# Turning one quadrant of w1 on VectorE instead of TensorE in a two-layer LoRA kernel on one core, with two adapter products and x's rows in another order

## The chip, the cores and the metric

One core of a Trainium2 chip runs the program. The metric is the device time in microseconds (us), median of several executions. The program is one launch, and all arithmetic of the reference is done on the core.

## The reference

Two residual linear layers follow each other, each with a low-rank adapter picked by an index; x is 8 x 256 x 1024 in float32.

```
x = x + x @ W0.T + (x @ lora_A[label]) @ lora_B.T * 0.5
x = x + x @ W1.T + bias + (x @ lora_As[slot]) @ lora_Bs[slot] * 2
```

The layers have 1024 inputs and outputs. The adapter ranks are 32 and 16.

## The kernel before, in words

**One matrix for two layers.** With an identity added to each weight (a for W0, b for W1 turned over), the two layers are one product with V = a·b plus low-rank terms. The kernel first makes V, once, and then takes 8 batches of 256 rows of x through it. Both the making of V and the batches use a Winograd-type scheme over 2 x 2 quadrants of 512 x 512: sums S1 to S4 of a's quadrants, T1 to T4 of b's, seven products of which each is `row_product` or `by_halves`. In the trace the sums and their parts are s, t, the results v, vt, m.

**Three products for one.** Each float32 operand is split in a high part, which ScalarE makes by a rounding copy (`high`), and a low part, which VectorE makes as a difference (`low`). TensorE then does hi·hi, hi·lo and lo·hi, each a 128x512 matmul (`step`, L1262 on).

**b's quadrants have to be turned.** w1 lies as rows of outputs, and b11, b12, b22 and b21 are wanted with inputs on the partitions. `turn` (L1217) does it with four 128x128 transposes on TensorE for each 128 columns, into a bank of PSUM; ScalarE and VectorE read the bank. b21 is the last: `turn_b21` is called three times between the halves of the product S2·T2 and once within the second half (L1352 to L1356). From the bank ScalarE copies `b21_hi` and `b21` (L543 to L546), VectorE makes `b21_lo` (`b21_low`, L898).

**The order ahead of the product A12·B21.** After S2·T2 TensorE runs, in this order: q's first half with B21, the adapter's c with A11 and A12 (`c_first`), b0·a1 (8 matmuls with 256 columns), and q's second half with T3 and B22. All orders are written out by hand, engine by engine, with semaphores between them. The order on VectorE at that place is `a1_lo`, `a1d`, two `b21_low`, `t4_sum(0)`, two `b21_low`, four `low` of a12, `t4_sum(1)`, and so on.

**Where the later steps meet.** ScalarE takes c's first half out of PSUM (`ct`), then makes `s1_hi` twice, then takes out b0·a1 (`q_part`); VectorE sums that into `b0a1_all` and goes on with `s1_low`. Further on, four rounds of `vt23(m)` (vt2, then vt3) and `turn_x` follow on VectorE. ScalarE makes vt2_hi and vt3_hi of each round and only after the last one copies c's second half (`ct[:, H:D]`), which TensorE waits for (`ct_made`, 2) after the first quarter of S1·T1, before it turns ct. In batch 0, TensorE waits for `u_lo_made` (`u_low` on VectorE) before the product with `p_hi` that adds the low-rank term.

**x's rows.** `turn_x` (L962) turns x by 32x32 blocks on VectorE; row 8·sl + 2·sb + odd of a batch goes to column 4·sl + sb of `xt`, so that a block of 32 results is written with a step of four elements. The store puts partition p to row 2·p + odd.

```
nc.vector.transpose(xt[:, n, :, :].rearrange("p e (s sb) -> p sb e s", sb=GR).bitcast(I32),
                    rows[:, n // 2, n % 2].bitcast(I32)).then_inc(xt_made, 1)
```

**Loads.** All are on SyncE's queue, in order: the quadrants of w1 and W0 in pairs, then n21 (raw w1 quadrant 21, 4 DMAs with pieces of 512 bytes), a12, a1 (8 DMAs, one per batch, after the index is known), a0, and x once `q_done` is 1.

Of the kernel before, what the change touches and what calls it, by code (L numbers as in the profile page):

```python
# [5 lines left out]
F32 = mybir.dt.float32  # L6
# [14 lines left out]
def two_layer_lora_kernel(nc, x, label0, slot1, w0, a0, b0w, w1, bias, a1, b1, out):  # L21
# [45 lines left out]
    n21 = at("n21", [P, HK, HK, P], F32, 20 * SLOT)  # L67
# [84 lines left out]
    with ExitStack() as ctx:  # L152
        bank = [ctx.enter_context(nc.psum_tensor(f"bank{n}", [P, 512], F32)) for n in range(8)]

        def sem(name):
            return ctx.enter_context(nc.semaphore(name))
# [4 lines left out]
        n21_in = [sem(f"n21_in{j}") for j in range(HK)]  # L161
# [27 lines left out]
        T22_AT, T12_AT, T21_AT = (4, 5, 8, 9), (6, 7, 10, 11), (12, 13, 14, 15)  # L189
# [47 lines left out]
        TURN_BANK = [bank[n] for n in (6, 7, 4, 5, 6, 7, 4, 5, 6, 7, 4, 6, 7, 4, 6, 7)]  # L237
        TURNED_THERE = {4: 0, 5: 1, 6: 2, 7: 3, 8: 4, 9: 5, 10: 6, 11: 8, 12: 9, 13: 10, 14: 11, 15: 12}
# [16 lines left out]
        def last_half(h):  # L255
            dst = out[B - 1, :, sides[h]].rearrange("(p odd) i -> odd p i", odd=2)
            return dst[0], y[:, C11, sides[h]]
# [6 lines left out]
        def _(sp):  # L264
# [201 lines left out]
        def _(act):  # L466
# [94 lines left out]
            for h in range(2):  # L561
                high(b22_hi, b22, PAIR[h], w1_hi_made)
# [153 lines left out]
        def _(dve):  # L716
# [144 lines left out]
            def t4_sum(h):  # L861

                dve.wait_ge(t2_made, h + 1)
                dve.wait_ge(w1_made, 2 * HK + 2 * h + 2)
                tt(t4[:, PAIR[h], :], b21[:, PAIR[h], :], t2[:, PAIR[h], :], ALU.subtract, t4_made)
# [24 lines left out]

            raw_a1 = a1_raw[:, :, :, :].rearrange("p t b r -> p t (b r)")
# [4 lines left out]
            tt(a1d[:, :, :], raw_a1[:, HK:KT, :], raw_a1[:, 0:HK, :], ALU.subtract, a1d_made)  # L896

            def b21_low(j):  # L898
                dve.wait_ge(w1_made, 2 * HK + j + 1)
                tt(b21_lo[:, j, :], TURN_BANK[T21_AT[j]][:, :], b21_hi[:, j, :].bitcast(F32), ALU.subtract, w1_lo_made)  # L900

            b21_low(0)
            b21_low(1)
            t4_sum(0)
            b21_low(2)
            b21_low(3)
# [3 lines left out]
            t4_sum(1)  # L910
            q_half(0)
            b22_low(0)
            b22_low(1)
# [20 lines left out]
            p_low(1)  # L934
# [15 lines left out]
            v11_sum(0)  # L950
            a22_low(0)
            a22_low(1)
            v11_sum(1)
            v11_sum(2)
# [5 lines left out]
            for m in range(HK):  # L960
                v11_low(m)
# [240 lines left out]
        def _(pe):  # L1202
# [8 lines left out]
            def row_tile(tile, j, m):  # L1211
# [4 lines left out]
                     + [(t1_made, 1), (t1_made, 2)] + [(w1_made, HK + 3), (w1_made, HK + 4)]  # L1216
                     + [(t1_made, 3), (t1_made, 4)] + [(w1_lo_made, HK + 1)])  # L1217
# [154 lines left out]
            for j in range(HK):  # L1372
                q_step(Q_BANK[1], j, T3, j, j == 0, False)
            pe.wait_ge(w1_lo_made, 2 * HK + 2)
            for j in range(HK):
                last = q_step(Q_BANK[1], KT + j, B22, j, False, j == HK - 1)
            last.then_inc(q_done, 1)
# [222 lines left out]
```

## Time and profile before

| what | value |
|---|---|
| median of 3 runs | 294.67 us (294.54 to 294.78) |
| the profiled execution, device time | 294.32 us |
| its span, first to last instruction | 292.6 us |
| granted TensorE clock, mean | 1.000 |
| TensorE matmul busy | 288.8 us, 99% |
| VectorE busy | 242.8 us, 83% |
| ScalarE busy | 153.9 us, 53% |
| GpSimd busy | 30.4 us, 10% |
| HBM read, written | 20.59 MB, 8.39 MB |

A timeline row gives the start in us from the span's start, the length in us, engine, line, operation, output<-input by name, and the idle time before it with what ended it. Matmuls overlap: a 128x512 one is shown with 0.39 us, and the next one starts 0.23 us after it. On VectorE and ScalarE too the next instruction starts some 0.1 us before the shown end of the last, if it waits for nothing.

### The profile page before, as it was taken

How to read it: one execution, taken by the hardware profiler on the slowest of the kernel's cores; microseconds unless marked ns; L12 is line 12 of the kernel's file. 1: busy time of each engine (PE TensorE's matmuls, PEld its weight loads, DVE VectorE, ACT ScalarE, POOL GpSimd, SP SyncE). 2: the span in 40 equal slices, each digit the busy share in tenths (PEclk: the TensorE clock that was granted, in tenths of full speed). 3: DMA queues.
4: the chain of work that ended last, by engine and by line, in shares of the span. 5: the costliest groups of instructions: out<-in, count | busy, mean ns of one | idle time of the engine just before them, and what ended most of it. 6: DMA issues, size and time to landing. Idle time of an engine off the chain costs nothing.

```text
span 292.6 us, 4450 instructions
## 1 busy us (share of the span) xinstructions
PE 288.8 (99%) x1337; PEld 236.0 (81%) x1337; DVE 242.8 (83%) x368; ACT 153.9 (53%) x270; POOL 30.4 (10%) x81
## 2 busy tenths in 40 slices
PE   8999999999999999999999999999999999999996
PEld 6888888888888888878878878878878878878885
DVE  3789996999999999999996897797798698695432
ACT  3685576879257537464453463373364355355120
POOL 1718100010000501000100100100100100100000
DMA  6999420800006600093268076068068159013004
GB/s 203 323 322 325 51 37 10 137 1 2 0 0 110 98 27 1 5 148 136 46 100 217 22 130 188 18 103 220 3 108 214 16 103 237 0 36 145 0 1 146
DMA packets 100803, 29.17 MB, mean 100 GB/s; under 512 B 85548, under 2 KB 93996, under 8 KB 100788
## 3 DMA queue, kind: packets, MB, share of 16 engines
q1 hardware_dynamic: 100788, 28.99, 42.7%
q8 instruction: 7, 0.11, 0.2%
q14 instruction: 8, 0.07, 0.1%
HBM read 20.59 MB, written 8.39 MB: 99 GB/s over the span
## 4 chain that ended last, share of the span: by engine, by line
PE 99%; ACT 0%; DVE 0%; issue 0%
PE bank L1204 94%; PE bank L1228 3%; PE bank L1450 1%; PE bank L1416 0%; ACT b_hi L468 0%; DVE y L718 0%
## 5 line engine op out<-in xcount | busy, mean ns | idle before, releaser
L1204 PE MATMUL bank<-v_hi,lhs 128*128 128x512 f32 (+1 forms) x136 | 42.5, 377 | 0.0
L1204 PE MATMUL bank<-vt_hi,s_hi 128*128 128x512 f32 x96 | 37.3, 389 | 0.0
L1204 PE MATMUL bank<-vt_lo,s_hi 128*128 128x512 f32 x96 | 37.3, 389 | 0.0
L1204 PE MATMUL bank<-vt_hi,s_lo 128*128 128x512 f32 x96 | 37.3, 389 | 0.0
L969 DVE STREAM_TRANSPOSE xt<-raw 128x512 int32<-128x512 int32 x32 | 32.4, 1076 | 1.4 <-DMA raw<-in_x 1.4
L1204 PEld LDWEIGHTS bank<-v_hi,lhs 128*128 128x128 f32 x136 | 25.1, 188 | 4.5
L468 ACT ACTIVATE lhs<-xt 128x512 fp32r<-128x512 f32 x32 | 19.6, 626 | 13.0 <-PE bank L1204 12.7
L1204 PE MATMUL bank<-v_lo,lhs 128*128 128x512 f32 (+1 forms) x68 | 25.7, 378 | 0.0
L1204 PE MATMUL bank<-vt_hi,lhs 128*128 128x512 f32 x64 | 22.1, 406 | 0.0
L718 DVE TENSOR_TENSOR lhs<-xt,lhs 128x512 fp32r<-128x512 f32 x32 | 21.7, 686 | 0.3
L434 POOL CAST ac<-c_hi 128x128 fp32r (+1 forms) x16 | 7.2, 450 | 135.5 <-PE bank L1204 98.5
L718 DVE TENSOR_TENSOR s_lo<-s_sum,s_hi 128x512 fp32r<-128x512 f32 x32 | 21.1, 682 | 0.2 <-ACT s_hi L468 0.2
L1204 PEld LDWEIGHTS bank<-vt_lo,s_hi 128*128 128x128 f32 x96 | 18.0, 188 | 3.7
L1204 PEld LDWEIGHTS bank<-vt_hi,s_hi 128*128 128x128 f32 x96 | 18.0, 188 | 3.7
L1204 PEld LDWEIGHTS bank<-vt_hi,s_lo 128*128 128x128 f32 x96 | 18.0, 188 | 3.7
L468 ACT ACTIVATE s_hi<-s_sum 128x512 fp32r<-128x512 f32 x32 | 19.1, 624 | 2.1 <-DVE s_sum L718 1.8
L1204 PE MATMUL bank<-t_hi,s_hi 128*128 128x512 f32 x48 | 19.1, 397 | 0.0
L1204 PE MATMUL bank<-t_hi,s_lo 128*128 128x512 f32 x48 | 18.7, 390 | 0.0
L1204 PE MATMUL bank<-t_lo,s_hi 128*128 128x512 f32 x48 | 18.7, 389 | 0.0
L468 ACT ACTIVATE u_part<-bank 64x256 f32<-64x256 f32 x8 | 3.1, 382 | 28.0 <-PE bank L1204 28.0
L718 DVE TENSOR_TENSOR y<-bank,u_sum 128x512 f32<-128x512 f32 x16 | 11.0, 685 | 6.3 <-PE bank L1204 6.3
L468 ACT ACTIVATE vt_hi<-vt 128x512 fp32r<-128x512 f32 x16 | 10.1, 630 | 10.9 <-DVE vt L718 10.5
(167 smaller groups left out, 662.6 us busy)
## 6 DMA issues: line engine op xcount, KB each, us to landing
raw<-in_x SPq DMA_DIRECT2D x32, 256.0 KB, 4.9
out<-y SPq DMA_DIRECT2D x31, 256.0 KB, 2.7
n<-in_L_cond_W SPq DMA_DIRECT2D x16, 256.0 KB, 5.3
a<-in_L_cond_W SPq DMA_DIRECT2D x16, 256.0 KB, 5.2
a_raw<-in_L_cond_lora_A SPq DMA_DIRECT2D x8, 128.0 KB, 2.4
b_raw<-in_L_cond_lora_Bs SPq DMA_DIRECT2D x16, 64.0 KB, 2.1
e_raw<-in_L_cond_lora_Bs SPq DMA_DIRECT2D x32, 32.0 KB, 1.8
a_raw<-in_L_cond_lora_As SPq DMA_DIRECT2D x8, 64.0 KB, 2.4
```

Of the source, the lines that this page charges most:

```text
L434: nc.gpsimd.tensor_copy(ac[:, :, at_col:at_col + R1], c_hi[:, :, cols].bitcast(F32)).then_inc(ac_c_made, 1)
L468: nc.scalar.activation(out_ap, in_ap, COPY, scale=scale).then_inc(made, 1)
L718: nc.vector.tensor_tensor(out_ap, one, other, op).then_inc(made, 1)
L969: nc.vector.transpose(xt[:, n, :, :].rearrange("p e (s sb) -> p sb e s", sb=GR).bitcast(I32), rows[:, n // 2, n % 2].bitcast(I32)).then_in ...
L1204: return nc.tensor.matmul(ps, lhsT, rhs, start=start, stop=stop, skip_group_check=more)
L1228: last = nc.tensor.transpose(ps[:, P * t:P * t + P], tile[:, j, t, :], eye[:, :])
L1450: return nc.tensor.matmul(ps, e_st[rows, P * t:P * t + P], e_p[rows, cols], start=False, stop=True, skip_group_check=True, tile_position=( ...
```

## The change

w1's quadrant 21 is loaded by 16 DMAs instead of 4, in pieces of 32 numbers (128 bytes), so that groups of 32 columns stand on the partitions that they need; four transposes by 32x32 blocks on VectorE then give b21. TensorE's 16 transposes and ScalarE's four copies `b21` are gone. `b21_low` reads b21 in place of a bank. On TensorE q's second half with T3 goes ahead of q's first half with B21, and the one with B22 goes between the two halves of c, all ahead of b0·a1. a1 is loaded ahead of a12. On VectorE both `t4_sum` stand after the first `v11_sum`, `a1d` after a12's lows, `p_low(1)` after `v11_sum(0)`, vt2's first sum ahead of v11's lows. x's rows go to columns 32·sb + sl instead of 4·sl + sb, and the stores put them back with a matching pattern.

```diff
-            for j in range(HK):
-                load_n(n21, 0, 1, j, n21_in[j])
-            for j in range(HK):
-                load_a(a12, 0, 1, j, a12_in[j])
+            w1_21 = w1[0:H, H:D].rearrange("(nb sl) (j g r) -> j g sl nb r", sl=32, g=GR, r=32)
+            for j in range(HK):
+                for g in range(GR):
+                    sp.dma_start(n21[32 * g:32 * g + 32, j, :, :], w1_21[j, g]).then_inc(n21_in, 16)
...
+            for j in range(HK):
+                load_a(a12, 0, 1, j, a12_in[j])
...
-                    "o (p odd) i -> odd (o p) i", odd=2)
+                    "o (sl sb odd) i -> odd (o sb) sl i", sb=GR, odd=2)
...
+            for j in range(HK):
+                act.wait_ge(w1_made, 2 * HK + j + 1)
+                high(b21_hi, b21, j, w1_hi_made)
             act.wait_ge(a1_in, 16 * B)
             copy(a1_hi[:, :, :], a1_raw[:, :, :, :].rearrange("p t b r -> p t (b r)"), a1_hi_made, LORA1_SCALE)
-            for j in range(HK):
-                act.wait_ge(turned, T21_AT[j] + 1)
-                bank_copy(b21_hi, j, TURN_BANK[T21_AT[j]], w1_hi_made)
-                bank_copy(b21, j, TURN_BANK[T21_AT[j]], w1_made)
             act.wait_ge(v_done, M6 + HK)
+            for h in range(2):
+                high(b22_hi, b22, PAIR[h], w1_hi_made)
...
+            dve.wait_ge(n21_in, 64 * HK)
+            dve.wait_ge(v_done, M7 + HK)
+            for j in range(HK):
+                nc.vector.transpose(b21[:, j, :].bitcast(I32),
+                                    n21[:, j, :, :].rearrange("p nb r -> p (nb r)").bitcast(I32)).then_inc(w1_made, 1)
...
-                    nc.vector.transpose(xt[:, n, :, :].rearrange("p e (s sb) -> p sb e s", sb=GR).bitcast(I32),
+                    nc.vector.transpose(xt[:, n, :, :].rearrange("p e (sb s) -> p sb e s", sb=GR).bitcast(I32),
...
-                    if h == 1 and m == 2:
-                        turn_b21(HK - 1)
-                if h == 0:
-                    for j in range(HK - 1):
-                        turn_b21(j)
+            pe.wait_ge(t1_made, HK)
+            pe.wait_ge(w1_made, 2 * HK)
+            for j in range(HK):
+                q_step(Q_BANK[1], j, T3, j, j == 0, False)
             for j in range(HK):
                 pe.wait_ge(w1_lo_made, HK + j + 1)
                 last = q_step(Q_BANK[0], HK + j, B21, j, False, j == HK - 1)
             last.then_inc(q_done, 1)
             pe.wait_ge(a1_lo_made, 1)
-            pe.wait_ge(w1_made, 3 * HK)
             c_first(0, A11)
+            pe.wait_ge(w1_lo_made, 2 * HK + 2)
+            for j in range(HK):
+                last = q_step(Q_BANK[1], KT + j, B22, j, False, j == HK - 1)
+            last.then_inc(q_done, 1)
             pe.wait_ge(w0_lo_made, 2 * HK)
             c_first(1, A12).then_inc(ct_done, 1)
```

VectorE, from the last low part of S2 to the sums of b0·a1, before (b_58 is b21, n_69 is n21, t_75 T2, t_81 T4, s_93 S4, b_64 b22, a_55 a12; a_st is a1_lo):

```order
L718 TENSOR_TENSOR s_lo<-s_87,s_hi 128x1024
L893 SCALAR_TENSOR_TENSOR a_st<-a_raw,a_st 128x8x128
L718 TENSOR_TENSOR a1d<-a_raw 128x512
L718 TENSOR_TENSOR b_lo<-bank,b_hi 128x512 x2
L718 TENSOR_TENSOR t_81<-b_58,t_75 128x1024
L718 TENSOR_TENSOR b_lo<-bank,b_hi 128x512 x2
L718 TENSOR_TENSOR a_lo<-a_55,a_hi 128x512 x4
L718 TENSOR_TENSOR t_81<-b_58,t_75 128x1024
```

The same place now:

```order
L720 TENSOR_TENSOR s_lo<-s_87,s_hi 128x1024
L896 STREAM_TRANSPOSE b_58<-n_69 128x512 x4
L720 TENSOR_TENSOR b_lo<-b_58,b_hi 128x512 x4
L909 SCALAR_TENSOR_TENSOR a_st<-a_raw,a_st 128x8x128
L720 TENSOR_TENSOR b_lo<-b_64,b_hi 128x1024 x2
L720 TENSOR_TENSOR a_lo<-a_55,a_hi 128x512 x4
L720 TENSOR_TENSOR a1d<-a_raw 128x512
```

Four transposes have come in, and the two sums T4 have gone from here. VectorE again, from q's second half to the first round of vt, now (v_99 is V11, vt_110 vt2, vt_113 vt3):

```order
L806 SCALAR_TENSOR_TENSOR q<-bank,q_part 32x512
L720 TENSOR_TENSOR s_lo<-s_93,s_hi 128x1024 x2
L720 TENSOR_TENSOR v_99<-bank,m_96 128x512
L720 TENSOR_TENSOR p_hi<-q,p_hi 32x512
L720 TENSOR_TENSOR t_81<-b_58,t_75 128x1024 x2
L720 TENSOR_TENSOR v_99<-bank,m_96 128x512 x2
L720 TENSOR_TENSOR a_lo<-a_61,a_hi 128x1024 x2
L720 TENSOR_TENSOR t_lo<-t_72,t_hi 128x1024 x2
L720 TENSOR_TENSOR v_99<-bank,m_96 128x512
L720 TENSOR_TENSOR t_lo<-t_81,t_hi 128x1024 x2
L720 TENSOR_TENSOR vt_110<-bank,m_97 128x512
L720 TENSOR_TENSOR v_lo<-v_99,v_hi 128x512 x4
```

Both sums T4 now stand behind the first v_99, and the four v_lo behind the first vt_110; what follows is as before.

## Rows read from the trace of the kernel before

**Rows 1.** The page: span, and the chain that ended last.

```profile
span 292.6 us, 4450 instructions
...
PE 99%; ACT 0%; DVE 0%; issue 0%
```

**Rows 2.** Waits of TensorE: who waited for whom, us in total, times, longest.

```profile
PE bank L1204 <- PEq L1589: 0.8, 1, 0.8
```

**Rows 3.** Timeline of TensorE around b21's transposes; start us, length us.

```profile
39.74 1.47 PE L1228 MATMUL bank<-eye,n 128*128 128x128 f32 x12
40.97 0.48 PE L1204 MATMUL bank<-t_hi,s_hi 128*128 128x512 f32 x1
...
45.19 0.60 PE L1228 MATMUL bank<-eye,n 128*128 128x128 f32 x4
45.54 0.48 PE L1204 MATMUL bank<-t_hi,s_hi 128*128 128x512 f32 x1
45.86 0.39 PE L1204 MATMUL bank<-t_lo,s_hi 128*128 128x512 f32 x1
```

**Rows 4.** Timeline of VectorE, from S2's last low part to the fourth round of vt.

```profile
38.82 1.23 DVE L718 TENSOR_TENSOR s_lo<-s,s_hi 128x1024 fp32r<-128x1024 f32 x1
...
43.09 1.22 DVE L718 TENSOR_TENSOR t<-b,t 128x1024 f32<-128x1024 f32 x1
...
58.00 0.27 DVE L923 SCALAR_TENSOR_TENSOR b0a_all<-bank,q_part 32x128 f32<-32x128 f32 x1
...
65.84 2.36 DVE L718 TENSOR_TENSOR a_lo<-a,a_hi 128x1024 fp32r<-128x1024 f32 x2 [0.68 <-ACT a_hi L468]
...
74.46 2.49 DVE L718 TENSOR_TENSOR v_lo<-v,v_hi 128x512 fp32r<-128x512 f32 x4
...
82.70 1.08 DVE L969 STREAM_TRANSPOSE xt<-raw 128x512 int32<-128x512 int32 x1
83.64 0.67 DVE L718 TENSOR_TENSOR vt<-bank,m 128x512 f32<-128x512 f32 x1
84.34 0.69 DVE L718 TENSOR_TENSOR vt<-vt,v 128x512 f32<-128x512 f32 x1
```

**Rows 5.** Timeline of TensorE: b0·a1, start of A12·B21, ct's transposes.

```profile
54.27 1.12 PE L1204 MATMUL bank<-a_st,b_st 128*128 128x256 f32 x8
...
58.88 0.39 PE L1204 MATMUL bank<-b_hi,a_hi 128*128 128x512 f32 x1
...
88.80 1.03 PE L1416 MATMUL bank<-eye,ct 128*128 128x128 f32 x8
```

**Rows 6.** Timeline of ScalarE at c's two halves.

```profile
54.53 0.60 ACT L468 ACTIVATE ct<-bank 128x512 f32<-128x512 f32 x1 [0.91 <-PE bank L1204]
...
57.05 0.27 ACT L468 ACTIVATE q_part<-bank 32x128 f32<-32x128 f32 x1
...
84.34 1.36 ACT L468 ACTIVATE vt_hi<-vt 128x512 fp32r<-128x512 f32 x2 [0.89 <-DVE vt L718]
86.28 0.60 ACT L468 ACTIVATE ct<-bank 128x512 f32<-128x512 f32 x1 [0.57 <-PE bank L1204]
```

**Rows 7.** Timeline of VectorE in batch 0, up to u_low.

```profile
116.60 0.42 DVE L718 TENSOR_TENSOR u_sum<-bank,u_part 64x256 f32<-64x256 f32 x1 [0.32 <-ACT u_part L468]
...
117.39 1.08 DVE L969 STREAM_TRANSPOSE xt<-raw 128x512 int32<-128x512 int32 x1
118.50 0.42 DVE L718 TENSOR_TENSOR u_st<-u_sum,u_st 32x256 fp32r<-32x256 f32 x1
...
123.66 0.48 DVE L1057 SCALAR_TENSOR_TENSOR u_st<-hh,low_mask,u_sum 32x256 fp32r<-32x256 f32 x1
```

**Rows 8.** Timeline of TensorE in batch 0: the product that waits for u_low.

```profile
124.29 0.63 PE L1204 MATMUL bank<-p_hi,u_st 128*128 128x512 f32 x2
```

**Rows 9.** Timeline of SyncE's issues: n21, x.

```profile
18.55 3.25 SPq L272 DMA_DIRECT2D n<-in_L_cond_W  x4
...
49.02 6.30 SPq L305 DMA_DIRECT2D raw<-in_x  x4
```

More of the change, by code:

```diff
@@ L66, in two_layer_lora_kernel @@
     n11 = at("n11", [P, HK, HK, P], F32, 12 * SLOT)
-    n21 = at("n21", [P, HK, HK, P], F32, 20 * SLOT)
+    n21 = at("n21", [P, HK, H // 32, 32], F32, 20 * SLOT)
     n22 = at("n22", [P, HK, HK, P], F32, 16 * SLOT)
@@ L160, in two_layer_lora_kernel @@
         n11_in = [sem(f"n11_in{j}") for j in range(HK)]
-        n21_in = [sem(f"n21_in{j}") for j in range(HK)]
+        n21_in = sem("n21_in")
         n22_in = [sem(f"n22_in{j}") for j in range(2)]
@@ L183, in two_layer_lora_kernel @@
         c_hi_made, c_lo_made = sem("c_hi_made"), sem("c_lo_made")
-        T22_AT, T12_AT, T21_AT = (4, 5, 8, 9), (6, 7, 10, 11), (12, 13, 14, 15)
+        T22_AT, T12_AT = (4, 5, 8, 9), (6, 7, 10, 11)
         n_eyed, w0_eyed, turned = sem("n_eyed"), sem("w0_eyed"), sem("turned")
@@ L235, in two_layer_lora_kernel @@
         HIGH = [bank[5], bank[4], bank[7], bank[6]]
-        TURN_BANK = [bank[n] for n in (6, 7, 4, 5, 6, 7, 4, 5, 6, 7, 4, 6, 7, 4, 6, 7)]
-        TURNED_THERE = {4: 0, 5: 1, 6: 2, 7: 3, 8: 4, 9: 5, 10: 6, 11: 8, 12: 9, 13: 10, 14: 11, 15: 12}
+        TURN_BANK = [bank[n] for n in (6, 7, 4, 5, 6, 7, 4, 5, 6, 7, 4, 6)]
+        TURNED_THERE = {4: 0, 5: 1, 6: 2, 7: 3, 8: 4, 9: 5, 10: 6, 11: 8}
         Q_BANK = [bank[5], bank[6]]
@@ L255, in last_half @@
         def last_half(h):
-            dst = out[B - 1, :, sides[h]].rearrange("(p odd) i -> odd p i", odd=2)
+            dst = out[B - 1, :, sides[h]].rearrange("(sl sb odd) i -> odd sb sl i", sb=GR, odd=2)
             return dst[0], y[:, C11, sides[h]]
@@ L560, in _ @@
             q_half(0)
-            for h in range(2):
-                high(b22_hi, b22, PAIR[h], w1_hi_made)
             act.wait_ge(a1d_made, 1)
@@ L863, in t4_sum @@
                 dve.wait_ge(t2_made, h + 1)
-                dve.wait_ge(w1_made, 2 * HK + 2 * h + 2)
+                dve.wait_ge(w1_lo_made, HK + 2 * h + 2)
                 tt(t4[:, PAIR[h], :], b21[:, PAIR[h], :], t2[:, PAIR[h], :], ALU.subtract, t4_made)
@@ L889, in _, with b21_low @@
                 s2_low(h)
+            dve.wait_ge(n21_in, 64 * HK)
[3 more added lines that the diff above has]
+                                    n21[:, j, :, :].rearrange("p nb r -> p (nb r)").bitcast(I32)).then_inc(w1_made, 1)
+            def b21_low(j):
+                dve.wait_ge(w1_hi_made, HK + j + 1)
+                dve.wait_ge(w1_made, 2 * HK + j + 1)
+                low(b21_lo, b21, b21_hi, j, w1_lo_made)
+            for j in range(HK):
+                b21_low(j)
             raw_a1 = a1_raw[:, :, :, :].rearrange("p t b r -> p t (b r)")
@@ L895, in _ @@
                                            op1=ALU.subtract).then_inc(a1_lo_made, 1)
[L896 to L906, printed above, removed]
+            b22_low(0)
+            b22_low(1)
             for j in range(HK):
@@ L909, in _ @@
                 low(a12_lo, a12, a12_hi, j, w0_lo_made)
-            t4_sum(1)
+            tt(a1d[:, :, :], raw_a1[:, HK:KT, :], raw_a1[:, 0:HK, :], ALU.subtract, a1d_made)
             q_half(0)
-            b22_low(0)
-            b22_low(1)
             s4_sum(0)
@@ L933, in _ @@
                 low(s4_lo, s4, s4_hi, PAIR[h], vs_lo_made)
-            p_low(1)
             def t1_low(h):
@@ L950, in _ @@
             v11_sum(0)
+            p_low(1)
+            t4_sum(0)
+            t4_sum(1)
+            v11_sum(1)
+            v11_sum(2)
             a22_low(0)
             a22_low(1)
-            v11_sum(1)
-            v11_sum(2)
             t1_low(0)
@@ L959, in _ @@
             t4_low(1)
-            for m in range(HK):
-                v11_low(m)
             def turn_x(b, quarters):
@@ L968, in turn_x, with vt2_sum @@
                 for n in quarters:
-                    nc.vector.transpose(xt[:, n, :, :].rearrange("p e (s sb) -> p sb e s", sb=GR).bitcast(I32),
+                    nc.vector.transpose(xt[:, n, :, :].rearrange("p e (sb s) -> p sb e s", sb=GR).bitcast(I32),
                                         rows[:, n // 2, n % 2].bitcast(I32)).then_inc(xt_made, 1)
-            def vt23(m):
+            def vt2_sum(m):
                 dve.wait_ge(v_done, M3 + m + 1)
@@ L976, in vt23, with vt3_sum @@
                 tt(vt2[:, m, :], HIGH[m][:, :], m17[:, m, :], ALU.add, vt2_made)
+            def vt3_sum(m):
                 dve.wait_ge(vt2_made, m + 1)
@@ L986, in vt23_low @@
                 low(vt3_lo, vt3, vt3_hi, m, vt3_lo_made)
+            vt2_sum(0)
+            for m in range(HK):
+                v11_low(m)
             dve.wait_ge(q_done, 2)
             for m in range(HK):
-                vt23(m)
+                if m:
+                    vt2_sum(m)
+                vt3_sum(m)
                 turn_x(0, (m,))
@@ L1215, in _ @@
             taken = ([(w1_made, j + 1) for j in range(HK)] + [(w1_made, HK + 1), (w1_made, HK + 2)]
-                     + [(t1_made, 1), (t1_made, 2)] + [(w1_made, HK + 3), (w1_made, HK + 4)]
-                     + [(t1_made, 3), (t1_made, 4)] + [(w1_lo_made, HK + 1)])
+                     + [(t1_made, 1), (t1_made, 2)] + [(w1_made, HK + 3), (w1_made, HK + 4)])
             def turn(tile, j, n, eyed=0):
@@ L1241, in turn_b12 @@
                 turn(n12, j, T12_AT[j])
-            def turn_b21(j):
-                pe.wait_ge(n21_in[j], 16)
-                turn(n21, j, T21_AT[j])
             def step(ps, a, b, j, m, start, stop, more=False):
@@ L1371, in _ @@
             last.then_inc(b0a1_done, 1)
-            for j in range(HK):
[L1373 to L1377, printed above, removed]
             for m in range(HK):
```

## The prediction, made before the changed kernel had run

> **What bounds the kernel now.** I read the page first: TensorE is the whole chain that ended last, 99% [rows 1]. Then its waits: 0.8 us, at the very start [rows 2]. So TensorE never waits, and its idle time tells nothing; what counts is the distance from one matmul's start to the next. From the start of A12·B21 to the transposes of ct stand 132 matmuls of 128x512, in 88.80 - 58.88 = 29.92 us [rows 5], 0.227 us each: a stream without a gap. Whatever leaves this stream is gained, whatever makes it wait is lost one for one, so I look for the instruction of another engine that TensorE would now meet. Those are in the timelines of VectorE and ScalarE [rows 4, 6, 7]. VectorE waits little between 40 and 116 us: it is nearly as full there as TensorE is.
>
> The profiled execution took 294.32 us for a span of 292.6 us; the median of the runs is 294.67. All shifts below are against the profiled execution's own times, and I add their sum to the median.
>
> **1. The transposes leave TensorE.** The first twelve take from 39.74 to 40.97, 1.23 us; four more take 45.19 to 45.54, 0.35 us; after each of the two groups the first matmul holds the stream 0.32 us (45.54 to 45.86) in place of 0.227, 0.09 more [rows 3]. Sum 1.23 + 0.35 + 0.18 = 1.76 us gained.
>
> **2. The cover that they gave.** The second half of S2·T2 waits for S2's last low part, which ends on VectorE at 38.82 + 1.23 = 40.05 [rows 4]. It was hidden behind the twelve transposes; now TensorE stands there at 39.74. With some 0.1 us for the semaphore it starts at 40.15: 0.4 lost. Left: 1.3 (1.36, less the few hundredths that matmuls are slow after a break). Everything on TensorE then stands 1.3 earlier: A12·B21 starts at 57.6, the wait for ct comes at 88.80 - 1.3 = 87.5.
>
> **3. b21 from VectorE.** Four transposes and four lows run from 40.05 on. At the price of x's transposes (0.94 from start to start, 82.70 to 83.64 [rows 4]) they end at 43.8 and the lows, 0.60 each, at 46.2. TensorE now has q with T3 ahead (8 matmuls, 1.8 us) and takes the first part of B21 at 47.4. The ScalarE copies between run beside the transposes, and its four copies `b21` are off a queue that isn't the bound. Cost 0; without q with T3 ahead it would be about 1 us. The lows, a1_lo (1.2, to 47.4) and b22's two (2.3, to 49.8) each come 1.5 us or more before TensorE asks.
>
> **4. The loads.** n21 now moves 1 MB in pieces of 128 bytes, which is what x's load is: 6.30 us of issues for 1 MB, against 3.25 for n21 in pieces of 512 bytes [rows 9]. So a1 comes some 3 us later, a12 behind it. n21 is issued by 18.55 + 6.3 = 25 us, or by 29 if the queue is still full; VectorE wants it at 40.05. a1 moves to about 41 and ScalarE takes it at 44; a12 is wanted at 48. GpSimd's steps don't move. Cost 0; upper bound below.
>
> **5. VectorE is held at b0·a1.** c's second half now ends right ahead of b0·a1. A12·B21 starts at 57.6; b0·a1's eight matmuls take 1.12 less the 0.17 by which a matmul is shown past its successor's start, 0.95, so they start at 56.65. Before, too, they followed c's end, and `ct` on ScalarE started 54.53 - 54.27 = 0.26 behind their start [rows 5, 6]: now at 56.9, and from `ct` to the end of `q_part` it is 57.05 + 0.27 - 54.53 = 2.79 us [rows 6]: 59.7. VectorE has nothing left by 57.1 and waits there for some 2.6 us, what it gained by its idle time at 45 us included. Before it began `b0a1_all` at 58.00 [rows 4]. Shift of VectorE: +1.7.
>
> **6. T4's sums stand behind that point.** Both t4_sum come into the stretch that follows, 1.13 each: +2.3 (the one at 43.09 [rows 4]). ScalarE's a22_hi is in time now, so the idle 0.68 goes, 0.8 with the overlap that a waiting instruction lacks; vt2's own round loses another 0.1. Shift of VectorE at the fourth round of vt: 1.7 + 2.3 - 0.8 - 0.1 = +3.1 us, if x's transposes cost what they did.
>
> **7. What one turn of x costs.** A turn takes 1.08 us where differences of the same 128x512 take 0.67 to 0.69 (from start to start 0.94 against 0.60, (2.49 - 0.69) / 3 [rows 4]). Before, it writes with a step of four elements; now it writes neighbours. The trace has no transposed block written densely, so its price lies between 0.60 and 0.94. I take 0.60: the transposes are the one VectorE form here with such a step and also the one that is dear. That is 0.34 less each. Three turns lie ahead of the fourth round of vt, four ahead of batch 0.
>
> The Trainium skill, "SBUF — State Buffer", section "Door 1: The DMA port swizzle", says that SBUF works in lines of 16 bytes and that accesses which move to a new line each time pay; by that the dense writes are cheap and the sum is the one that I take, without it the dear one below. No run here shows it yet.
>
> **8. First meeting: ct.** vt3 of the last round ended at 84.34 + 0.69 = 85.03. Shifted by 3.1 - 3·0.34 = 2.1 it ends at 87.1; vt3_hi follows, ct's copy some 0.52 later, 0.60 long [rows 6]: 88.3. TensorE wanted it at 87.5: 0.8 lost. It now stands at 88.3 against 88.80, 0.5 us ahead. (With turns as dear as before: 89.3, 0.5 behind.)
>
> **9. Second meeting: u_low in batch 0.** It ended at 123.66 + 0.48 = 124.14, and the product that waits for it started at 124.29 [rows 7, 8]: there was next to no room. VectorE comes with 3.1 - 4·0.34 = 1.7, loses its idle 0.32 [rows 7], and has four turns on the way, of which I count three as cheaper (the instruction behind the first one waits for ScalarE's `u0_hi_made` too): 124.14 + 1.7 - 0.3 - 1.0 = 124.55. TensorE comes at 124.29 - 0.5 = 123.8 and waits until 124.6. So TensorE is 0.3 us behind where it was, and stays there: from batch 1 on VectorE has idle time in every batch, and turns of x that are cheaper gain nothing against a full TensorE. Sum: +0.3 us, 295.0.
>
> **The rivals.**
>
> *Turns of x stay dear.* Mechanism: the price is that of the transpose and not of the step. Then VectorE is 3.1 late at ct and 3.1 - 0.3 = 2.8 late at u_low: 124.14 + 2.8 = 126.9, TensorE at 127.0, 2.7 behind: 297.4, slower by 0.9%. For it: every transpose in the trace is dear, and nothing shows a cheap one. Against: no other form writes with the step. In between, each 0.1 us of a turn is worth 0.7 us of the kernel. It decides from a turn of some 0.65 us on. Chance 0.22.
>
> The Trainium skill, "VectorE: DVE Perf Modes", section "The three transpose paths", has 311 ns for 128x128 in bf16; were float32 the same, that would be the price of an ordinary operation and speak against this rival.
>
> *Both waits stay hidden.* Mechanism: VectorE isn't held at b0·a1 as long as I make it, or runs closer; then only steps 1 and 2 count: -1.3 us, 293.4. It needs VectorE 1.5 us earlier at u_low than my sum. For it: my sum on VectorE is made of some forty instructions, and each may be a few hundredths off. Against: 1.5 is much more than that gives. Chance 0.10, with half of the gain in part of it.
>
> *The loads come late.* If the 16 issues run at the rate of a full queue, n21, a1 and a12 slip; the first to be met is ScalarE's a12_hi and then c's second half. Up to 3 us late, 296 to 298. It decides when a12 lands after 49. Chance 0.06.
>
> **How the numbers follow.** Forecast 0.62, the rivals 0.22, 0.10 and 0.06. A measurement of this kernel tells 0.2%, 0.6 us, from no change. The forecast's +0.3 has some 0.45 us around it (the semaphore in step 2, the price of a turn between 0.60 and 0.64, small waits on VectorE), so of its 0.62 about 0.40 lies within 0.2%, 0.18 above and 0.04 below. Slower: 0.18 + 0.21 + 0.06, less what of these falls inside, 0.43. Faster: 0.04 + 0.10, 0.14. Within: 0.43. Its own range is 294.2 to 295.8; the range given takes in the dear turns and half of the case of hidden waits: 293.8 to 297.6.
>
> **What would show it.** TensorE: no transposes with n; a first matmul at about 40.15 behind one at 39.5; 0.8 us lost ahead of ct's transposes and 0.8 ahead of the p_hi product in batch 0. VectorE: four b turns from 40.1 on; an idle time of 2 to 3 us that ScalarE's q_part ends, near 59.7; turns of x of about 0.69 us. If the turns read 1.08, the dear rival holds; if no wait stands before ct or before p_hi, the chain on VectorE is shorter than I have it. A wait for n21, a1 or a12 anywhere would make step 4 wrong.

## The result, and the profile after

The changed kernel takes **304.19 us** (303.7 to 304.46, 6 runs) against 294.71 us (294.54 to 294.85, 6 runs) of the kernel before on the same chip: ratio 1.0319, 95% interval 1.0306 to 1.0332. It is 9.5 us slower. The range given, 293.8 to 297.6, misses it by more than 6 us, and no rival gave such a time. The profiled execution took 304.3 us for a span of 302.6 us.

The page of the changed kernel: span, the chain that ended last by engine and then by line, and one row each of its group list and of its DMA issues (KB each, median us from issue to landing).

```profile
span 302.6 us, 4430 instructions
...
PE 48%; DVE 27%; issue 8%; DMA 7%; SPq 5%; ACT 2%; DVEq 0%; ACTq 0%
PE bank L1217 47%; DMA a_raw<-in_L_cond_lora_A 6%; DVE s_lo L720 4%; DVE vt_lo L720 3%; DVE t L720 3%; DVE t_lo L720 2%; DVE s L720 2%; DVE vt L720 2%; SPq L273 2%; DVE v L720 2%; DVE s_sum L720 2%; DMA a<-in_L_cond_W 2%; DVE xt L974 2%; DVE v_lo L720 1%; DVE lhs L720 1%
...
L974 DVE STREAM_TRANSPOSE xt<-raw 128x512 int32<-128x512 int32 x32 | 21.0, 688 | 0.0
...
out<-y SPq DMA_DIRECT2D x31, 256.0 KB
...
a_raw<-in_L_cond_lora_A SPq DMA_DIRECT2D x8, 128.0 KB, 8.5
```

In [rows 1] TensorE was 99% of the chain. Now half of the chain lies elsewhere, and 6% of it is one load, a0 (`a_raw`), which lands after 8.5 us. In the page of the kernel before the same load took 2.4, and a store 2.7; the changed kernel's page gives the stores no time to landing:

```profile
out<-y SPq DMA_DIRECT2D x31, 256.0 KB, 2.7
a_raw<-in_L_cond_lora_A SPq DMA_DIRECT2D x8, 128.0 KB, 2.4
```

TensorE's waits in the changed kernel, in the form of [rows 2]:

```profile
PE bank L1217 <- DVE u_st L1070: 2.0, 2, 1.5
PE bank L1217 <- PEq L1594: 0.8, 1, 0.8
PE bank L1217 <- DVE s_lo L720: 0.8, 1, 0.8
PE bank L1421 <- ACT ct L471: 0.6, 1, 0.6
```

Here is what the stages add, from starts of matmuls in the two timelines (the end from the span):

| from | to | before, us | after, us | more |
|---|---|---|---|---|
| span's start | first product | 5.53 | 6.00 | 0.47 |
| first product | batch 0's p_hi | 118.76 | 119.18 | 0.42 |
| batch 0's p_hi | last matmul | 165.15 | 167.85 | 2.70 |
| last matmul | span's end | 3.12 | 9.52 | 6.40 |

The sum is 10.0 us, all of it. What I predicted is the second row: 0.3 us forecast, 0.42 measured. The last two rows, 9.1 us, my sum did not have. Of the third row 2.6 us fall in batches 1 and 4 and 0.1 in batch 0; from batch to batch the other distances are those of the kernel before. (The first row is start-up: in the twelve kernels profiled here the first product starts between 5.24 and 6.00, and no edit goes with it.)

**The end.** SyncE's issues of stores, then the stretch behind them; the columns of the second block are busy time of each engine, the granted clock, the busy share of the 16 DMA engines, and GB/s.

```profile
288.12 3.62 SPq L342 DMA_DIRECT2D out<-y  x3
292.44 1.90 SPq L370 DMA_DIRECT2D out<-y  x2
```

```profile
292.00:294.00 2.00, 1.31 (x11) 1.11 (x10) 0.83 (x2) 0.00 (x0) 0.00 (x0) 1.00 0.26 101
294.00:298.00 4.00, 0.00 (x0) 0.00 (x0) 0.00 (x0) 0.00 (x0) 0.00 (x0) 0.77 0.26 102
298.00:303.00 5.00, 0.00 (x0) 0.00 (x0) 0.00 (x0) 0.00 (x0) 0.00 (x0) 0.50 0.18 66
```

The last issue ends at 294.34, the span at 302.55: 8.2 us in which nothing but stores runs, up to 298 at 102 GB/s and a DMA share of 0.26. Four engines of sixteen, all busy, would be a share of 0.25. (The view gives only the mean over the sixteen; that it is four of them is inferred, here and below.) In the kernel before the last issue ends at 290.55 and the span 2.0 us later:

```profile
288.85 1.70 SPq L367 DMA_DIRECT2D out<-y  x2
```

In the changed kernel TensorE's granted clock falls to 0.50 in this stretch, behind its last matmul; that costs nothing.

**The batches.** ScalarE, VectorE and TensorE in batch 1, and the chain of waits there:

```profile
147.59 0.42 ACT L471 ACTIVATE ac<-a_raw 128x256 fp32r<-128x256 f32 x1 [4.90 <-DMA a_raw<-in_L_cond_lora_A]
...
148.55 0.41 ACT L471 ACTIVATE hh<-u_sum 32x256 fp32r<-32x256 f32 x1
```

```profile
149.00 0.47 DVE L1070 SCALAR_TENSOR_TENSOR u_st<-hh,low_mask,u_sum 32x256 fp32r<-32x256 f32 x1 [2.29 <-ACT hh L471]
```

```profile
147.66 0.39 PE L1217 MATMUL bank<-v_hi,lhs 128*128 128x512 f32 x1
149.53 0.73 PE L1217 MATMUL bank<-p_hi,u_st 128*128 128x512 f32 x2 [1.48 <-DVE u_st L1070]
```

```profile
140.37 7.20 DMA a_raw<-in_L_cond_lora_A
...
206.09 10.03 DMA a_raw<-in_L_cond_lora_A
```

A wait in four links: the stores hold the DMA engines, a0 issued behind them lands late, `ac` holds ScalarE's queue and `hh` behind it, `u_low` on VectorE waits for `hh`, and TensorE for `u_low`. From matmul to matmul it is 1.87 us instead of 0.227 in batch 1 and 0.88 in batch 4. ScalarE waits for a0 in six of the eight batches (17.9 us in all), but only these two waits reach TensorE. Where the DMA engines stand, from windows of 2 us, first of the kernel before and then of the changed one:

```profile
136.00:138.00 2.00, 2.00 (x11) 1.65 (x10) 2.00 (x3) 0.00 (x0) 0.00 (x0) 1.00 0.80 300
138.00:140.00 2.00, 2.00 (x11) 1.65 (x10) 2.00 (x4) 0.38 (x1) 1.01 (x4) 1.00 0.41 66
140.00:142.00 2.00, 2.00 (x11) 1.65 (x10) 1.90 (x5) 1.43 (x4) 0.00 (x0) 1.00 0.00 0
```

```profile
136.00:138.00 2.00, 2.00 (x10) 1.65 (x9) 2.00 (x5) 0.60 (x1) 0.00 (x0) 1.00 0.24 38
138.00:140.00 2.00, 2.00 (x10) 1.69 (x9) 1.76 (x3) 0.21 (x1) 0.07 (x1) 1.00 0.21 60
140.00:142.00 2.00, 2.00 (x10) 1.65 (x10) 1.66 (x4) 0.97 (x3) 0.94 (x4) 1.00 0.44 132
```

Before, the stores go at 300 GB/s on 0.80 of the engines and are done by 140. After, the share stays at 0.21 to 0.24, near the 0.25 of four busy engines, and the stores last until the next loads come. The bytes moved there, 38 and 60 GB/s, are fewer than the 102 at the end, at nearly the same share; why isn't shown.

**The making stage** has the waits that were foreseen, not all in their sizes. TensorE at the three places of [rows 3], [rows 5] and [rows 8], then VectorE, to be read against [rows 4]:

```profile
40.05 0.39 PE L1217 MATMUL bank<-t_hi,s_lo 128*128 128x512 f32 x1
41.19 0.50 PE L1217 MATMUL bank<-t_hi,s_hi 128*128 128x512 f32 x1 [0.76 <-DVE s_lo L720]
...
88.33 0.39 PE L1217 MATMUL bank<-t_hi,s_lo 128*128 128x512 f32 x1
89.35 0.88 PE L1421 MATMUL bank<-eye,ct 128*128 128x128 f32 x6 [0.64 <-ACT ct L471]
...
125.18 0.50 PE L1217 MATMUL bank<-p_hi,u_st 128*128 128x512 f32 x1
```

```profile
41.05 2.48 DVE L896 STREAM_TRANSPOSE b<-n 128x512 int32<-128x512 int32 x4
43.46 2.45 DVE L720 TENSOR_TENSOR b_lo<-b,b_hi 128x512 fp32r<-128x512 f32 x4
...
60.73 0.28 DVE L928 SCALAR_TENSOR_TENSOR b0a_all<-bank,q_part 32x128 f32<-32x128 f32 x1 [2.99 <-ACT q_part L471]
```

TensorE stands before S2·T2's second half (1.14 us from start to start, 0.91 lost), before ct's transposes (0.8 lost) and before p_hi (0.26 lost). On VectorE b21's four transposes start at 41.05, and b0·a1's sum waits 2.99 us for `q_part`.

### The profile page after: what moved, and what is told of

It reads as the page before. It is cut to its first block, busy times and chain, and to the rows that moved or that the text cites. A ratio compares the mean times of both kernels' runs of the same rounds, so it can differ in the third digit from the quotient of the medians.

```text
span 302.6 us, 4430 instructions
## 1 busy us (share of the span) xinstructions
PE 288.9 (95%) x1321; PEld 234.2 (77%) x1321; DVE 233.9 (77%) x372; ACT 153.6 (51%) x266; POOL 29.9 (10%) x81
## 4 chain that ended last, share of the span: by engine, by line
PE 48%; DVE 27%; issue 8%; DMA 7%; SPq 5%; ACT 2%; DVEq 0%; ACTq 0%
PE bank L1217 47%; DMA a_raw<-in_L_cond_lora_A 6%; DVE s_lo L720 4%; DVE vt_lo L720 3%; DVE t L720 3%; DVE t_lo L720 2%; DVE s L720 2%; DVE vt L720 2%; SPq L273 2%; DVE v L720 2%; DVE s_sum L720 2%; DMA a<-in_L_cond_W 2%; DVE xt L974 2%; DVE v_lo L720 1%; DVE lhs L720 1%
## 5 line engine op out<-in xcount | busy, mean ns | idle before, releaser
L974 DVE STREAM_TRANSPOSE xt<-raw 128x512 int32<-128x512 int32 x32 | 21.0, 688 | 0.0
L720 DVE TENSOR_TENSOR u_sum<-bank,m_sum 128x512 f32<-128x512 f32 x8 | 5.5, 687 | 15.1 <-PE bank L1217 15.0
```

The costliest lines, as they stand in the source:

```text
L720: nc.vector.tensor_tensor(out_ap, one, other, op).then_inc(made, 1)
L974: nc.vector.transpose(xt[:, n, :, :].rearrange("p e (sb s) -> p sb e s", sb=GR).bitcast(I32), rows[:, n // 2, n % 2].bitcast(I32)).then_in ...
```

## The experiments

The theory after this reading (A, where an expectation names it by letter): the stores' pattern alone is the loss. `odd (o sb) sl i` has 4 as its outermost size, where `odd (o p) i` had 128, and the DMA then runs on four engines. Its rivals: the distance in the output between the rows of neighbouring partitions, which is 8 rows of 4 KB now and was 2, costs in itself (C), or the loss sits in what the prediction was about, VectorE and the loads.

**store4: the stores alone.** The kernel before with nothing changed but the two store patterns.

```diff
-                    "o (p odd) i -> odd (o p) i", odd=2)
+                    "o (sl sb odd) i -> odd (o sb) sl i", sb=4, odd=2)
...
```

> The kernel before with nothing changed but the stores' pattern, which is the changed kernel's: 4 groups of 32 partitions outermost (the output's rows come out in another order, the work is all there). Theory A, a store whose outermost dimension has 4 entries uses 4 of the 16 DMA engines: the last store ends some 6 us later than before (span from the last store's issue to the end 8 us in place of 2), a0's load lands late behind the stores and holds TensorE once or more ahead of the p_hi product; with dear turns of x VectorE has less room than in the changed kernel, so 301 to 304 us. Rival B, the loss sits in n21's loads, in the order of the adapter products or in VectorE's chain: within 0.3 us of before, 294.7. Rival C, the loss is the distance of the rows that a store writes one after the other (8 rows, not 2): as slow as A says.

Measured: 303.62 us (303.26 to 305.64), ratio 1.031 (1.0289 to 1.033). That is 8.9 us more than the kernel before, of the changed kernel's 9.5. a0 lands after 8.5 us, and TensorE stands before two p_hi products (1.97 us in batch 1, 1.79 in batch 5, from start to start). The profiled execution was the slowest of the five, 305.64: 6.8 us more than before behind the last matmul and 3.6 from batch 0's p_hi product to it.

**store16 and store8: the outermost size.** The same edit with `sb=16` and `sb=8`. These three kernels write the output's rows in another order.

> As store4, but 16 groups of 8 partitions outermost, with the rows that a group writes 32 rows apart. Theory A: 16 engines again, so within 0.5 us of before, 294.7, and 2 us from the last store's issue to the end. Rival B: 294.7 too. Rival C, the distance of the rows: as slow as store4 or slower, 301 or more.

> The kernel before with the stores' outermost dimension 8 (rows of the output in another order than the reference's). Theory (the DMA runs on as many of the 16 engines as that dimension has): 8 engines, so a store of 256 KB takes about half of what it takes with 4: span's end 3 to 4 us behind the last issue, against 8.3 with 4 and 2.1 with 16; a0's load lands in about 4 us. TensorE waits little or not for a0 in the batches: 296 to 297.5. Rival (the cost grows with the distance between rows and not with the engines): 8 rows' distance lies between the distances of 16 and 4, and since 16 and the neighbouring rows cost the same within 0.6 us, 8 would cost little: under 295.6.

Measured: store16 295.39 us (295.11 to 295.72), ratio 1.0021 (1.001 to 1.0033). store8 296.21 us (295.46 to 297.4), ratio 1.005 (1.0033 to 1.0066). A window near the end, of store8, of store4 and of store16:

```profile
291.00:292.00 1.00, 0.00 (x0) 0.00 (x0) 0.00 (x0) 0.00 (x0) 0.00 (x0) 1.00 0.52 197
```

```profile
295.00:298.00 3.00, 0.00 (x0) 0.00 (x0) 0.00 (x0) 0.00 (x0) 0.00 (x0) 1.00 0.26 101
```

```profile
290.00:291.00 1.00, 0.15 (x2) 0.00 (x0) 0.42 (x1) 0.00 (x0) 0.00 (x0) 1.00 0.72 223
```

| outermost size | kernel | last issue to span's end, us | DMA share in that window | a0 to landing, us | ratio |
|---|---|---|---|---|---|
| 4 | store4 | 8.6 | 0.26 | 8.5 | 1.031 |
| 8 | store8 | 4.2 | 0.52 | 3.2 | 1.005 |
| 16 | store16 | 2.4 | 0.72 | 2.4 | 1.0021 |
| 128 | before | 2.0 | | 2.4 | 1 |

Twice the size, half the time and twice the share, 0.26 and 0.52 where 4 and 8 busy engines of sixteen would give 0.25 and 0.50: I read 4 and 8 as numbers of engines. (store16's window lies ahead of its last issue's end, and not all of it is full.) The distance between rows is bounded by store16, where it is 32 rows, four times that of store4: 0.2% in all, 0.6 us. That rival falls. With store8 TensorE is never late in a batch; its loss is almost all behind the last matmul.

**oldrows: the change without its rows of x.** The changed kernel with x's rows, the turn and the stores of before. What is left is b21 on VectorE, the orders and the loads.

```diff
-                    nc.vector.transpose(xt[:, n, :, :].rearrange("p e (sb s) -> p sb e s", sb=GR).bitcast(I32),
+                    nc.vector.transpose(xt[:, n, :, :].rearrange("p e (s sb) -> p sb e s", sb=GR).bitcast(I32),
...
-                    "o (sl sb odd) i -> odd (o sb) sl i", sb=GR, odd=2)
+                    "o (p odd) i -> odd (o p) i", odd=2)
...
```

> The changed kernel with before's rows of x and before's stores: only b21 by VectorE and the new orders. Theory A and my prediction's steps: turns of x at 0.94, so TensorE waits some 1.8 us for ct and 2.2 us for u_low, and the kernel takes 297.4 (296.5 to 298). Theory D, that the stalls of the making stage were a minor matter and the making stage gains: 293.4 to 295. If the loss were in the new orders or n21's loads, 303 or more.

Measured: 298.61 us (297.87 to 299.91), ratio 1.0149 (1.0117 to 1.018); the profiled one took 297.87. This is my rival of dear turns, built: turns of 1.08 us, and both waits where it said and near the sizes expected (1.8 and 2.2 us lost were forecast; from start to start, less 0.227, they are 1.83 and 1.99). The time is over the range that I expected: +1.5%, where the rival said +0.9%. In the profiled execution, the fastest of the four, it is 3.2 us more from first product to last matmul, against 2.7 of the rival's sum; why the other three took longer isn't shown. First the group of the turns, then TensorE's waits:

```profile
L974 DVE STREAM_TRANSPOSE xt<-raw 128x512 int32<-128x512 int32 x32 | 32.5, 1080 | 0.9 <-DMA raw<-in_x 0.9
```

```profile
PE bank L1217 <- DVE u_st L1070: 1.8, 1, 1.8
PE bank L1421 <- ACT ct L471: 1.7, 1, 1.7
```

**fixrows: cheap turns, stores as before.** The changed kernel, with x's load split so that the dense turn leaves the rows in their natural order: 16 DMAs of 64 KB for a batch in place of 4 of 256 KB. The stores are those of before.

```diff
...
+                    for k in range(GR):
+                        src = x[bass.DynSlice(b, 1), 64 * k:64 * k + 64, :].rearrange(
+                            "o (sl odd) (t i) -> sl (o odd t) i", odd=2, i=P)
+                        dst = raw[32 * g:32 * g + 32, H * k:H * k + H]
...
-                    "o (sl sb odd) i -> odd (o sb) sl i", sb=GR, odd=2)
+                    "o (p odd) i -> odd (o p) i", odd=2)
```

> The changed kernel with its dense turns of x, but the rows are put in order by the load (16 DMAs of 64 KB per batch in place of 4 of 256 KB) and the stores are before's, 128 partitions outermost. Theory A: no loss at the end, a0 lands in 2.4 us, and what is left is my sum: 295.0 (294.2 to 296.2). If the loss is elsewhere than in the stores: 303 or more. A third way: the 16 issues for x hold SyncE's queue so long that stores or a0 are late: 297 or more, with waits for DMAs in the batches.

Measured: 295.53 us (294.64 to 296.02), ratio 1.0024 (1.0011 to 1.0037). This is nearly the forecast's own case, 295.0 (294.2 to 295.8), built; only x's load is not the changed kernel's. The waits stand before S2·T2's second half (1.6 us lost), before ct (0.8) and before p_hi in batch 0 (0.26), and none in the later batches, where every distance is that of the kernel before (15.78 us from the last p_hi product of a batch to the first of the next).

**split: all of the change, each store in four.** The changed kernel whole, with x's 4 DMAs and its row order; each store is four DMAs of 64 KB with 32 rows outermost.

```diff
-                sp.dma_start(dst[n // 2], y[:, n, :]).then_inc(y_out[n], 16)
+                for k in range(GR):
+                    sp.dma_start(dst[n // 2][k], y[32 * k:32 * k + 32, n, :]).then_inc(y_out[n], 16)
...
```

> The changed kernel with all its parts kept, x's rows and cheap load and the output's rows too, and each store of 256 KB made as four of 64 KB, one per block of 32 rows, so that the outermost dimension of each DMA is 32 in place of 4. Theory (the loss is the number of DMA engines that a store runs on, nothing else in the change): a0's load lands in 2.4 us, no wait of TensorE in batches 1 to 7, and the time is that of my sum, 295.0, and about 1.2 us for the four issues behind each of the last halves: 296.2 (295.3 to 297). Rival: the rows that stand 8 KB apart in the output cost in themselves; then the last store takes over 4 us to land and the time stays over 298.

Measured: 298.4 us (297.85 to 298.93), ratio 1.0134 (1.0118 to 1.015), outside of what I expected. The theory's part held, with the rows of the changed kernel and their distance of 8 kept: a0 lands in 2.3 us, no wait stands in a batch from 1 on, and from the first product to the last matmul it is 284.60 us, 0.69 more than before. What I had wrong is the end:

```profile
285.75 4.66 SPq L343 DMA_DIRECT2D out<-y  x10
290.45 3.69 SPq L372 DMA_DIRECT2D out<-y  x8
```

I had counted four issues behind the last half. But SyncE is still busy with the twelve issues ahead when the first half is ready (VectorE ends it at 289.2), so all eight come behind: 290.45 + 3.69 = 294.14, and the span ends 1.95 us later, at 296.09. The last store lands within 1.95 us, as the theory says; the issues are the loss at the end, 0.46 us each. The rival's condition (over 4 us to land; its "8 KB" was my slip, the rows are 32 KB apart) did not come true, although its time did.

**t4early: work into VectorE's idle time.** fixrows with both `t4_sum` ahead of the wait for b0·a1.

```diff
+            t4_sum(0)
+            t4_sum(1)
             dve.wait_ge(b0a1_part_made, 1)
...
```

> The kernel of the run fixrows with T4's two sums moved ahead of VectorE's wait for b0 a1, into the 3 us in which VectorE has nothing to do. By the sum of the prediction (VectorE is behind because T4's sums stand after that wait) VectorE comes 2.3 us earlier to everything behind it: the wait ahead of ct (1.03 us in fixrows) and the one ahead of p_hi in batch 0 (0.49 us) vanish, and the time falls by about 1.5 us, to 294.0. The wait for S2's low part (1.8 us between two matmuls' starts in fixrows) stays. Rival: VectorE doesn't decide, other engines (ScalarE's ct, vt3_hi) are as late without it; then the waits stay within 0.3 us and the time is that of fixrows, 295.5.

Measured: 294.09 us (293.65 to 294.71), ratio 0.9974 (0.9963 to 0.9985): a gain on fixrows of 0.5%, 1.4 us by the medians. TensorE's waits at ct and at u_low are gone from its list; VectorE's idle time (2.99 us in the changed kernel) is used, and 0.72 of it is left:

```profile
57.72 2.35 DVE L723 TENSOR_TENSOR t<-b,t 128x1024 f32<-128x1024 f32 x2
60.80 0.28 DVE L933 SCALAR_TENSOR_TENSOR b0a_all<-bank,q_part 32x128 f32<-32x128 f32 x1 [0.72 <-ACT q_part L474]
```

Steps 5 and 6 of the prediction together are the cause of both waits: this run does T4's sums inside the hold at b0·a1 instead of behind it, changes nothing else, and both waits go.

**qmid: the cover put back.** t4early with q's eight matmuls of T3 between the halves of S2·T2.

```diff
                     by_halves(h, S2, T2, m, v_done)
+                if h == 0:
+                    pe.wait_ge(t1_made, HK)
+                    pe.wait_ge(w1_made, 2 * HK)
+                    for j in range(HK):
+                        q_step(Q_BANK[1], j, T3, j, j == 0, False)
...
```

> t4early with q's eight matmuls of T3 (1.8 us) taken between the two halves of S2 T2, as a cover for the wait that the transposes covered in the kernel before. The wait for S2's low part (0.9 us lost in the changed kernel, 1.6 in fixrows) should be gone; if no other wait comes in its place the time is 1.3 to 1.8 us under the kernel before, 292.9 to 293.4: the gain of the transposes that left TensorE, whole. Rival: B21's low parts from VectorE are now met, since q's first matmuls no longer stand ahead of them: then a wait of up to 1.5 us stands ahead of q's B21 part and the time is that of t4early.

Measured: **292.84 us** (292.4 to 293.33), ratio 0.9927 (0.991 to 0.9945): 0.7% faster than the kernel before, and just under the time that I expected. VectorE's last low part of S2 ends as late as ever, and TensorE doesn't meet it. VectorE first, then TensorE:

```profile
40.46 1.23 DVE L723 TENSOR_TENSOR s_lo<-s,s_hi 128x1024 fp32r<-128x1024 f32 x1
```

```profile
40.40 0.39 PE L1220 MATMUL bank<-t_hi,s_lo 128*128 128x512 f32 x1
40.63 0.39 PE L1220 MATMUL bank<-t_hi,b_st 128*128 128x512 f32 x1
...
42.22 0.39 PE L1220 MATMUL bank<-t_lo,b_st 128*128 128x512 f32 x1
42.44 0.39 PE L1220 MATMUL bank<-t_hi,s_hi 128*128 128x512 f32 x1
```

From first product to last matmul it is 282.57 us against 283.91 before, 1.34 less.

**turnonly: cheap turns alone.** The kernel before with fixrows' load and dense turn.

```diff
...
-                    nc.vector.transpose(xt[:, n, :, :].rearrange("p e (s sb) -> p sb e s", sb=GR).bitcast(I32),
+                    nc.vector.transpose(xt[:, n, :, :].rearrange("p e (sb s) -> p sb e s", sb=GR).bitcast(I32),
```

> The kernel before with x's rows loaded in the order in which a dense turn leaves them natural (16 DMAs of 64 KB per batch in place of 4 of 256 KB), the dense turn, and the stores as they were. Turns should take 0.69 us in place of 1.08. Since TensorE never waited for VectorE in the kernel before, the time should be the same, 294.7 (within 0.5). Rival: 16 DMAs for each x cost something on the queue in the batches (SP issues the loads of adapters behind them); then it is slower, with a wait in the batches that names a load.

Measured: 295.66 us (294.57 to 296.33), ratio 1.0028 (1.0016 to 1.004), so the rival's slower time came and my expectation didn't hold; the load that a wait names is x's. The turns are cheap (0.69 us), but VectorE waits for x, and in the batches small waits of TensorE follow (0.58 us from start to start in batch 3; the stream of matmuls loses 1.6 us in all from batch 2 to batch 6). The group of the turns, and SyncE's issues:

```profile
L972 DVE STREAM_TRANSPOSE xt<-raw 128x512 int32<-128x512 int32 x32 | 21.0, 689 | 26.7 <-DMA raw<-in_x 26.7
```

```profile
169.69 11.84 SPq L308 DMA_DIRECT2D raw<-in_x  x16
```

With this load the cheaper turn gains nothing where TensorE is full; no run has the cheap turn with x's 4 DMAs on the kernel before. A load in 16 parts takes 11.8 us of the queue instead of 6.3 [rows 9]. That alone doesn't make TensorE wait: fixrows and qmid have the same load and no such wait. What tips it in turnonly isn't settled.

**splitbest: qmid's orders with x's four DMAs and the stores in four.** The edit is against qmid.

```diff
-                    for k in range(GR):
-                        src = x[bass.DynSlice(b, 1), 64 * k:64 * k + 64, :].rearrange(
-                            "o (sl odd) (t i) -> sl (o odd t) i", odd=2, i=P)
+                    src = x[bass.DynSlice(b, 1), :, :].rearrange("o (sl sb) (t i) -> sl (o sb t) i", sl=32, i=P)
...
-                sp.dma_start(dst[n // 2], y[:, n, :]).then_inc(y_out[n], 16)
+                for k in range(GR):
+                    sp.dma_start(dst[n // 2][k], y[32 * k:32 * k + 32, n, :]).then_inc(y_out[n], 16)
...
```

> The kernel of the run qmid with x's load as in the changed kernel (4 DMAs of 256 KB per batch in place of 16 of 64 KB) and the stores as four DMAs of 64 KB each. Theory: the same stream of TensorE as qmid (no wait for S2's low part, none at ct, none at u_low), and about 1.2 us more at the end for the issues: 294.0 (293.4 to 294.6). VectorE should wait under 5 us in all for x, against 21.8 in qmid, where x's 16 issues take 12 us. If the four issues hide behind each other at the end, it equals qmid, 292.8.

Measured: 296.1 us (295.57 to 296.34), ratio 1.0049 (1.0036 to 1.0062). The stream is as good as qmid's, 282.10 us from first product to last matmul, but the end takes 6.2 us where qmid's takes 3.1: the same eight issues as in split. I expected 294.0 before split's result was known; the two ran together, and the error is one and the same.

## Why the prediction was wrong, and what of it was right

**The step that failed** is the one that is missing. The sum has nine steps and none for the stores. Its only word on what comes after batch 0 is in step 9: TensorE "is 0.3 us behind where it was, and stays there". The diff changes two patterns of the stores, and the section on the change says that they "put them back with a matching pattern"; I took a matching permutation for a free one and costed it at nothing, without a row, without bounds and without a rival. It measured 8.9 us (store4's 303.62 against 294.7); in the changed kernel's trace 6.4 us stand at the end and 2.6 in two of the batches. The profile's list of DMA issues was there to be read: the stores' row says 256 KB in 2.7 us, and a window of a batch shows 0.80 of the engines at work for it. 300 GB/s at that share are 94 for four engines (an estimate from that window), so the 1.05 MB that the last batch stores would take 11 us. They are issued within 6.2 us (288.12 to 294.34), which leaves 5 behind the last issue, and the 2 that a store takes to land anyway: 7 us, of the 8.2 measured. The price was to be had from the trace, and would have been the largest term of the sum. That it is four engines, no row of the kernel before shows: every store there has 128 outermost.

A rule would have led to the four. The Trainium skill, "DMA: Bandwidth & Descriptors", section "Rules for kernel authors", says that the slowest dimension of the patterns sets the number of DMA engines, and that with an outermost size under 16 a DMA gets no more engines than that size; the section "Why a DMA increments its semaphore by 16 and not by 1" gives the count as the largest number up to 16 that divides both sides' outermost sizes. These runs agree: a share of 0.26 with 4, 0.52 with 8; the split stores, with 32 outermost, land after 1.6 us, and a0 behind them after 2.3.

The other steps, by their numbers:

1. **Transposes gone, 1.76.** Right. splitbest and qmid, in which no wait stands at S2's low part, ct or u_low, have 1.81 and 1.34 us less between first product and last matmul.
2. **Cover lost, 0.4.** The mechanism right, the size not: 0.9 in the changed kernel, 0.7 in oldrows, 1.1 in split and t4early, 1.6 in fixrows. S2's low part ended on VectorE at 41.14 instead of 40.05. It is not the change that moved it. From the first product on, its end stands at 34.52 us in the trace that I read, at 34.89 to 35.40 in the traces of store8, store16, turnonly and store4, which have the same making stage, and at 35.14 in the changed kernel. I had reckoned with the earliest of them, from one execution. Most of the difference is there by VectorE's first sum of a's quadrants, which starts at 15.41 in the kernel before and between 15.71 and 16.88 in all others; from there on VectorE has hardly a gap. Before, then the changed kernel:

```profile
15.41 1.23 DVE L718 TENSOR_TENSOR s<-a,a 128x1024 f32<-128x1024 f32 x1 [1.51 <-PE bank L1228]
```

```profile
16.26 1.23 DVE L720 TENSOR_TENSOR s<-a,a 128x1024 f32<-128x1024 f32 x1 [1.82 <-DMA a<-in_L_cond_W]
```

Why the first loads land at other times from run to run stays open.

3. **b21 from VectorE, 0.** Right; its transposes took 0.69 each, at a distance of 0.60, less than the 0.94 I had allowed, since they too write densely.
4. **The loads, 0.** Right in cost, wrong in size: I took n21's 16 issues at the price of x's 4, 6.3 us; they took 13.4 (0.84 each) and ended at 32.8 against 25 to 29. a1 came later by it and cost VectorE 0.69 us of idle time, which reached no wait of TensorE.
5. **VectorE held at b0·a1.** Foreseen 2.6 us idle, ended by `q_part` at 59.7; measured 2.99 us, at 60.73, which without the start-up of 0.47 is 60.26. The mechanism is right; nearly all of the 0.56 is step 2's error (0.5), passed on by TensorE.
6. **T4's sums behind it.** Right, shown by t4early.
7. **Turn of x at 0.60 from start to start.** Right: 0.69 shown, 0.60 to 0.63 apart, and 1.08 with a step (oldrows). The rule cited there (the Trainium skill, "SBUF — State Buffer", section "Door 1: The DMA port swizzle") agrees with these two rows: only the step differs between the two kinds of turn.
8. **ct, 0.8 lost.** The wait is right, 89.35 - 88.33 less 0.227, or 0.8; the place isn't. The forecast had TensorE 0.5 us ahead of the kernel before at this point; it stands at 83.35 us from the first product against 83.27, 0.1 behind. Both sides of the meeting were late by step 2's error.
9. **u_low, 0.3 behind.** TensorE is 0.42 behind at p_hi without the start-up, so the sum is nearly right, but not its parts. The wait was to be 0.8 and is 0.26, since TensorE came 0.6 later than forecast. u_low ended at 125.13, or 124.66 without the start-up, against 124.55 forecast: VectorE, 0.6 late at vt's fourth round (88.15, without the start-up 87.68, against 87.1), took some 0.5 less than I had counted from there on. Two errors of about half a microsecond cancel; that is luck. The last sentence of the step, that TensorE stays where it is, is the one that failed.

Of the rivals, the dear turns were true of a kernel with turns that write with a step; the two waits were priced nearly right, the time too low (+0.9% against oldrows' +1.5%). None covered what happened. All were about the same engines, those that I had been watching.

## What to carry to other kernels

Every line of a diff gets a term in the sum, a changed access pattern above all: a permutation that leaves the bytes as they are can still cut the stores from 300 GB/s to 101. Read the outermost size of both sides, and see in the profile's DMA share whether a stretch stands flat at a quarter or a half. When rows must be permuted, do it where the outermost size stays 16 or more (here in the load of x), and count what extra issues cost on the queue: hidden in a batch, dear at the end. Don't trust one trace for a small margin: where a meeting has 0.4 us of room or loss, read it in more than one (S2's low part scattered by 0.9 us among kernels with the same making stage). Work that leaves the engine that bounds takes a cover with it; put something else there in the same step (qmid: 1.2 us on top of t4early).

## What the runs showed of the hardware that I had not expected

- A store's DMA share follows its outermost size: 256 KB stores ran at 101 GB/s and a share of 0.26 with 4, at 197 GB/s and 0.52 with 8.
- Stores with 4 outermost delay a load issued behind them on the same queue: a0 took 8.5 us instead of 2.4, in windows in which the mean DMA share was 0.21 to 0.46.
- An int32 transpose by 32x32 blocks over 128x512 costs 0.69 us when it writes neighbours, as an ordinary difference does, and 1.08 us with a step of four elements.
- Issues of 64 KB cost SyncE 0.46 us (stores, rows of 2 KB) and 0.67 to 0.84 us (x and n21, in pieces of 128 bytes), against 0.52 (stores, four in 2.06 us in qmid) and 1.6 for 256 KB: four small ones take 1.7 to 3.5 times as long as one large.
